# Softmax of the last two cross-attention sequences: exponential before the transpose on ScalarE, clamp on GpSimd, one VectorE pass

## The reference

```python
attn = jnp.einsum('bhqd,bhkd->bhqk', q, k) * scale
attn = jnp.clip(attn, -CLAMP, CLAMP)          # CLAMP = 10000.0
attn = jax.nn.softmax(attn, axis=-1)
x = jnp.einsum('bhqk,bhkd->bqhd', attn, v).reshape(B, Nq, Cq)
return x @ Wo + bo
```

## Time and profile before

| | us |
|---|---|
| median of 3 runs | 1427.64 |
| lowest, highest | 1421.79, 1428.75 |
| profiled execution, its own time | 1431.25 |
| its span | 1429.4 |
| TensorE, VectorE busy | 1290.2, 915.3 |
| ScalarE, GpSimd busy | 572.9, 730.1 |

### The profile page before, as it was taken

One profiled execution on the slowest core, in us unless ns is written; L12 is line 12 of the kernel. 1 busy time (PEld: TensorE's weight loads), 2 busy tenths in 40 slices (PEclk: granted clock), 3 DMA queues, 4 the chain that ended last, 5 costly groups with the idle time before them and its releaser, 6 DMA issues.

```text
span 1429.4 us, 23660 instructions
## 1 busy us (share of the span) xinstructions
PE 1290.2 (90%) x9073; PEld 1098.9 (77%) x9073; DVE 915.3 (64%) x2305; ACT 572.9 (40%) x1172; POOL 730.1 (51%) x697
## 2 busy tenths in 40 slices
PE   6997999999999999999999989998773799999970
PEld 6996788888888888886777767776653799999970
DVE  3665622642272253235688878878765799999966
ACT  3567311121121121113545535544432576777732
POOL 3543566666576666634211242343434347888832
PEclk9998999999999999999999999999875899999995
DMA  6101223233343323310534343434713656666605
GB/s 188 36 22 35 74 89 108 91 115 91 118 133 96 96 88 104 92 62 25 155 93 132 90 81 117 97 88 131 232 43 110 190 198 224 222 231 233 229 18 168
DMA packets 63104, 169.56 MB, mean 119 GB/s; under 512 B 11029, under 2 KB 30735, under 8 KB 55056
## 3 DMA queue, kind: packets, MB, share of 16 engines
q1 hardware_dynamic: 52432, 122.19, 29.1%
q0 software_dynamic: 10560, 45.86, 9.1%
HBM read 138.57 MB, written 33.38 MB: 120 GB/s over the span
## 4 chain that ended last, share of the span: by engine, by line
PE 69%; DVE 16%; issue 4%; DMA 3%; ACT 3%; POOL 3%; SPq 1%; another core or an unknown queue 1%; ACTq 0%; POOLq 0%; DVEq 0%
PE bank L460 15%; PE bank L462 15%; PE bank L461 14%; PE bank L1350 6%; PE bank L468 5%; PE bank L1188 3%; PE bank L1107 3%; DVE shiftE L1873 2%; DVE shiftE L1867 2%; PE bank L1175 2%; PE bank L1266 1%; PE bank L1201 1%; DVE w_lo L1935 1%; DVE gh_hi L2010 1%; DVE x_tok L2033 1%
## 5 line engine op out<-in xcount | busy, mean ns | idle before, releaser
L1733 DVE CAST hid_hi<-bank 128x512 fp32r<-128x512 f32 x96 | 66.4, 691 | 254.9 <-ACT bank L1465 253.8
L602 POOL TENSOR_TENSOR wpiece_lo<-wraw,wpiece_hi 128x1024 fp32r<-128x1024 f32 x88 | 212.3, 2413 | 7.3
L462 PE MATMUL bank<-hid_hi,wpiece_hi 128*128 128x512 f32 x512 | 201.5, 394 | 0.0
L461 PE MATMUL bank<-hid_lo,wpiece_hi 128*128 128x512 f32 x512 | 200.2, 391 | 0.0
L460 PE MATMUL bank<-hid_hi,wpiece_lo 128*128 128x512 f32 x512 | 199.8, 390 | 0.0
L600 POOL TENSOR_SCALAR wpiece_hi<-wraw 128x1024 fp32r<-128x1024 f32 x88 | 93.9, 1067 | 154.4 <-PE bank L462 128.4
L1465 ACT ACTIVATE bank<-bank,ffn_scales 128x512 f32<-128x512 f32 x64 | 42.4, 662 | 304.4 <-PE bank L462 304.4
L461 PEld LDWEIGHTS bank<-hid_lo,wpiece_hi 128*128 128x128 f32 x512 | 96.1, 188 | 22.1
L460 PEld LDWEIGHTS bank<-hid_hi,wpiece_lo 128*128 128x128 f32 x512 | 96.1, 188 | 21.5 <-DVE hid_lo L1735 0.8
L462 PEld LDWEIGHTS bank<-hid_hi,wpiece_hi 128*128 128x128 f32 x512 | 96.2, 188 | 20.0
L460 PE MATMUL bank<-xgT_hi,w_lo 128*128 128x256 f32 x368 | 107.3, 292 | 1.8 <-DVE xgT_lo L1943 1.8
(11 more groups left out here) (342 smaller groups left out, 3589.3 us busy)
## 6 DMA issues: line engine op xcount, KB each, us to landing
wraw<-in_C_w SPq DMA_DIRECT2D x88, 512.0 KB, 3.6
w2raw<-in_F_w SPq DMA_DIRECT2D x8, 1152.0 KB, 7.3
w1raw<-in_F_w SPq DMA_DIRECT2D x8, 1028.0 KB, 7.0
split_qk<-qk_hi SPq DMA_DIRECT2D x64, 128.0 KB, 2.7
xt_lo<-split_qk SPq DMA_DIRECT2D x8, 1024.0 KB, 4.8
xt_hi<-split_qk SPq DMA_DIRECT2D x8, 1024.0 KB, 5.3
split_qk<-qk_lo SPq DMA_DIRECT2D x32, 128.0 KB
split_qk<-ctx_raw SPq DMA_DIRECT2D x32, 128.0 KB, 2.4
```

Of the source, the lines that this page charges most:

```text
L461: pe.e.matmul(o, sh, ml, start=False, stop=False)
L462: made = pe.e.matmul(o, sh, mh, start=False, stop=stop and i == n - 1)
L602: pool.e.tensor_tensor(pair[1], raw, f(pair[0]), ALU.subtract).then_inc(done, 1)
```

## The change

For the pairs of sequences 6 and 7 (`ALONE = B - 2`) the softmax is divided in another way. VectorE clamps from below only, into `shift_e`, and writes the maximum of each row over the first score in PSUM; a small operation turns the four maxima into -scale * min(max, lim), in `top_e`. ScalarE then takes the exponential of the rows in `shift_e`, four instructions with this as bias, in place. TensorE transposes the exponentials. ScalarE copies them to `prob_e` with no function. GpSimd bounds them to 0 to 1 in place, one instruction of 128x1024 per pair, and TensorE's product with the values waits for that. The upper clamp is so made after the exponential. On ScalarE the new step stands in the round of step 0 with priority 2.5. On GpSimd the new step stands in the round of step 1 with priority 0.5. Sequences 0 to 5 are as before. Two semaphores for fills are made one.

```diff
+ALONE = B - 2
@@ PLACE
+    "act": {("PAIR", 0): 2.5},
@@ pool_program
+                elif name == "PAIR" and step == 1 and args[0] >= ALONE:
+                    b, p = args
+                    u, pr = use["E", "p", b, p, 1], prob_e[(b * PAIRS + p) % 3].rearrange("p i k s -> p (i k s)")
+                    pool.wait_ge(u.drained, u.done)
+                    pool.e.tensor_scalar(pr, pr, 1.0, 0.0, ALU.min, ALU.max).then_inc(s_prob, 1)
@@ tensor_program
-                    for pair in (p - 1, p):
-                        shown = use["E", "p", b, pair, 1]
-                        pe.wait_ge(shown.drained, shown.done)
+                    if b >= ALONE:
+                        pe.wait_ge(s_prob, n + 1 - ALONE * PAIRS)
+                    else:
+                        for pair in (p - 1, p):
+                            shown = use["E", "p", b, pair, 1]
+                            pe.wait_ge(shown.drained, shown.done)
@@ scalar_program
+                elif name == "PAIR" and step == 0 and args[0] >= ALONE:
+                    b, p = args
+                    n, u = b * PAIRS + p, use["E", "s", b, p]
+                    act.wait_ge(u.drained, u.done)
+                    for m in range(2 * TT):
+                        sh = shift_e[n % 3][:, m, :]
+                        made = act.e.activation(sh, sh, ACT.Exp, scale=scale_e, bias=top_e[n % 3][:, m:m + 1])
+                    made.then_inc(s_shift, 1)
...
-                        act.e.activation(prob_e[n % 3][:, i, :, :], u.ap[:, :].rearrange("p (k s) -> p k s", k=TT), ACT.Exp,
-                                         scale=scale_e).then_inc(u.drained, 1)
+                        made = u.ap[:, :].rearrange("p (k s) -> p k s", k=TT)
+                        if b >= ALONE:
+                            act.e.activation(prob_e[n % 3][:, i, :, :], made, ACT.Identity).then_inc(u.drained, 1)
+                        else:
+                            act.e.activation(prob_e[n % 3][:, i, :, :], made, ACT.Exp, scale=scale_e).then_inc(u.drained, 1)
@@ vector_program
+                    if b >= ALONE:
+                        for m in range(2 * TT):
+                            made = dve.e.tensor_scalar(shift_e[n % 3][:, m, :], scores[:, m, :], -lim, -lim, ALU.max, ALU.max,
+                                                       accum_out=scores[:, m, 0:1])
+                        dve.mark(made)
+                        dve.wait_own()
+                        dve.e.tensor_scalar(top[:, :], scores[:, :, 0], lim, -scale_e, ALU.min, ALU.mult).then_inc(u.drained, 1)
+                        continue
```

More of the change, by code:

```diff
@@ L347, in build @@
         s_xdve, s_xpool, s_wqkv, s_bw, s_before = sem("xdve"), sem("xpool"), sem("wqkv"), sem("bw"), sem("before")
-        s_const, s_rtmem, s_none, s_vz = sem("const"), sem("rtmem"), sem("none"), sem("vz")
+        s_const, s_rtmem, s_none, s_vset = sem("const"), sem("rtmem"), sem("none"), sem("v_set")
         s_u, s_conv, s_nm, s_phi = sem("a_u"), sem("a_conv"), sem("a_nm"), sem("a_phi")
@@ L406, in build @@
         s_xb, s_cthi = {k: sem(f"xb_{k}") for k in "DE"}, {k: sem(f"ct_hi_{k}") for k in "DE"}
-        s_vone, s_shift = sem("ones"), sem("e_shift")
+        s_shift, s_prob = sem("e_shift"), sem("e_prob")
         s_qkhi, s_qklo, w_qk, l_qk = sem("e_qkhi"), sem("e_qklo"), ring(2, lambda i: sem(f"w_qk{i}")), ring(2, lambda i: sem(f"l_qk{i}"))
@@ L619, in pool_program @@
             for v in vpad:
-                pool.e.memset(v[:, :, :], 0.0).then_inc(s_vz, 1)
+                pool.e.memset(v[:, :, :], 0.0).then_inc(s_vset, 1)
             pool.e.memset(ones[:, :], 1.0).then_inc(s_const, 1)
@@ L689, in pool_program @@
                 pool.wait_own()
-                pool.e.memset(v[:, :, :, DH:DH + 1], 1.0).then_inc(s_vone, 1)
+                pool.e.memset(v[:, :, :, DH:DH + 1], 1.0).then_inc(s_vset, 1)
             for name, step, args in DE["pool"]:
@@ L1367, in scalar_program @@
                             if b < 2:
-                                act.wait_ge(s_vz, 2)
+                                act.wait_ge(s_vset, 2)
                             elif k == "v":
@@ L1778, in values @@
                     dve.wait_ge(last.filled, last.full)
-                dve.wait_ge(s_vone, 3)
+                dve.wait_ge(s_vset, 5)
                 dve.wait_ge(u.filled, u.full)
```

## The result

| | median, us | lowest to highest | ratio to before, 95% interval |
|---|---|---|---|
| before | 1424.92 | 1418.85 to 1428.98 | |
| changed | 1429.12 | 1423.72 to 1435.29 | 1.0031 [1.0019, 1.0044] |
| changed, again, beside the experiments | 1433.97 | 1429.29 to 1438.61 | 1.0028 [1.0005, 1.0051] |

The change costs 4.4 us (1429.12 x 0.0031), inside the 0.5% that the prediction calls no change. The forecast was 1433.2 us in 1422 to 1442, 5.6 above the 1427.64 from which it started. Of the 4.1 us between forecast and measurement, 2.7 come from that start (before has a median of 1424.92 over its 20 runs here), the rest from the change. The profiled execution of the changed kernel took 1423.72 us, span 1421.9, the fastest of its runs; that of before took 1431.25, above the highest of the 20 runs of before here.

The account below looks back on a forecast made before the run. It took VectorE as fullest near sequences 6 and 7, and the change to make a 3.5 us loop through ScalarE. Terms 2.3 - 0.4 + 1.3 + 0 + 1.2 + 1.2 = 5.6 us gave 1433.2, range 1422 to 1442.

## What to carry over

An engine at half load isn't free time for work that sits in a loop: count the hand-overs around it (block, transposes, copies, block) and compare that loop with the present round, not the busy shares. Relieving the bound was worth 8 us here and the place the work went to cost 12 to 13. And where a stretch of the trace holds a wait that nothing explains, work out what the step costs with it and without it, give both as the range, and take it as cover for what is added ahead of it.

## What the runs showed of the hardware

- ScalarE, 128x256 from SBUF to SBUF with a constant scale and a bias by row: 0.50 us for one, 0.40 from start to start; 128x512 from PSUM 0.60, two in 1.09.
- VectorE's read of the accumulator takes 0.14 us to PSUM and 0.08 to SBUF, and the pass before it starts every 0.38 instead of 0.345 us.
- GpSimd bounds 128x1024 in 1.04, 128x512 in 0.61 and 128x1 in 0.18 us, as the profile has it.
- A signal of TensorE can come microseconds after the recorded end of its matmuls: that of the acc_E transposes ahead of (7,0) 3.2 and 3.4 us in the two profiles of before and 4.5 without the bound, where most come within 0.1 us. The profile calls such a wait remote.
- 48 or 49 matmuls of the step (7,0) to (7,1) take 6.3 us at a granted clock of 0.73, 7.9 at 0.57 and 8.7 at 0.51.
